# Less of x stored, absolute sums as the bound of W, and the differences of batch 0 spread and loaded back by halves, around a seven-product matrix stage

## The reference, cut to what matters

```python
# x: (2, 1024, 2048), ctx: (2, 2048, 2048), float32
q1 = fake_quant(layernorm(x)); q2 = fake_quant(ctx)        # 8-bit grids
x = x + q1 @ q2                                            # per batch
n = layernorm(x)
w = top-2 router weights of softmax(n @ W_router.T)        # 8 experts
lora = sum over experts of w * ((n @ A_e.T) @ B_e.T) * 2   # rank 16 each
x = x + n @ W_base.T + b_base + lora
```

## Time and profile before

| | |
|---|---|
| median of 3 runs | 1152.16 us (1151.45 to 1152.73) |
| the profiled execution | 1155.63 us |
| its span in the trace | 1153.7 us |
| PE busy | 1005.7 us, 87% |
| DVE busy | 813.3 us, 70% |
| ACT busy | 433.7 us, 38% |
| DMA | 202.41 MB, 175 GB/s over the span |
| chain that ended last, largest | PE L1619 21%; DMA xd<-x_kept 5%; DMA spread<-scratch 4%; DMA w_r<-in_w_n 3% |

### The profile page before, as it was taken

How to read it: one execution, slowest core, us unless ns; L and a number is a source line. 1 busy time by engine, 2 the same in 40 slices (tenths; PEclk the granted TensorE clock), 3 DMA queues, 4 the chain that set the end, 5 groups by cost and what they waited for, 6 DMA issues and landing times.

```text
span 1153.7 us, 15006 instructions
## 1 busy us (share of the span) xinstructions
PE 1005.7 (87%) x5847; PEld 533.5 (46%) x5847; DVE 813.3 (70%) x1503; ACT 433.7 (38%) x428; POOL 18.7 (2%) x40
## 2 busy tenths in 40 slices
PE   0489778699899999898989889998596999999997
PEld 0356455466568943343433434443242444444443
DVE  6667776677663885677777675577339888888985
ACT  3779576676642222222332231123112232223220
POOL 0000000000000000000000000000000000000000
PEclk9899989899899999999999999999797999999999
DMA  8737787767664245466666655531953323323311
GB/s 318 283 140 257 245 274 261 231 219 235 229 219 149 81 130 135 153 198 228 207 219 213 231 180 150 193 96 64 291 192 128 101 91 133 122 80 118 132 47 45
DMA packets 69070, 202.41 MB, mean 175 GB/s; under 512 B 8153, under 2 KB 20489, under 8 KB 62729
## 3 DMA queue, kind: packets, MB, share of 16 engines
q1 hardware_dynamic: 67144, 199.35, 50.2%
q0 software_dynamic: 1280, 2.12, 1.7%
q10 hardware_dynamic: 576, 0.00, 0.0%
HBM read 159.46 MB, written 41.98 MB: 175 GB/s over the span
## 4 chain that ended last, share of the span: by engine, by line
PE 26%; DVE 16%; DMA 16%; issue 6%; ACT 4%; SPq 1%; ACTq 0%; POOL 0%; DVEq 0%; POOLq 0%
PE pair L1619 21%; DMA xd<-x_kept 5%; DMA spread<-scratch 4%; DMA w_r<-in_w_n 3%; DVE w_p L1086 3%; DMA scratch<-w_max 3%; DVE wst L1050 2%; PE pair L1596 2%; PE pair L1575 2%; ACT w_p L703 1%; DVE xd_p L1272 1%; ACT w_r L694 1%; PE pair L1565 1%; SPq L567 1%; DVE sq L1251 1%
## 5 line engine op out<-in xcount | busy, mean ns | idle before, releaser
L1596 PE MATMUL pair<-x2p,w_p 128*128 128x512 f16 x1536 | 345.8, 386 | 0.2
L1460 PE MATMUL pair<-q1T,ctx_q 128*128 128x342 f16 x1536 | 245.4, 323 | 7.4 <-DVE xt L887 7.4
L1596 PEld LDWEIGHTS pair<-x2p,w_p 128*128 128x128 f16 x1536 | 152.6, 99 | 189.1 <-issue 13.3
L1460 PEld LDWEIGHTS pair<-q1T,ctx_q 128*128 128x128 f16 x1536 | 153.6, 101 | 91.6 <-issue 9.0
L1619 PE MATMUL pair<-x2p,w_slot 128*128 128x512 f16 x768 | 173.1, 385 | 3.6 <-DVE u L1336 3.6
L1619 PEld LDWEIGHTS pair<-x2p,w_slot 128*128 128x128 f16 x768 | 76.0, 99 | 97.6 <-issue 5.3
L887 DVE SCALAR_TENSOR_TENSOR xt<-pair,par,xt 128x342 f32<-128x342 f32 (+1 forms) x96 | 54.4, 567 | 64.9 <-DMA xt<-in_xT 59.5
L694 ACT ACTIVATE w_r<-w_r 128x1024 f32<-128x1024 f32 x32 | 33.8, 1057 | 176.2 <-DVE wst L1050 176.2
L1575 PE MATMUL pair<-hwT,b_p 128*128 128x512 f16 x192 | 54.8, 396 | 42.8 <-ACT sq L719 31.8
L631 ACT ACTIVATE ctx_u<-ctx_f,par 128x2048 uint8<-128x2048 f32 x32 | 66.9, 2090 | 63.3 <-DMA ctx_f<-in_ctx 63.1
L1619 PE MATMUL pair<-x2p,x2p 128*128 128x512 f16 x336 | 77.0, 389 | 11.3 <-issue 11.3
(11 more groups left out here) (196 smaller groups left out, 1066.6 us busy)
## 6 DMA issues: line engine op xcount, KB each, us to landing
ctx_f<-in_ctx SPq DMA_DIRECT2D x32, 1024.0 KB, 7.1
rows<-in_x SPq DMA_DIRECT2D x16, 1024.0 KB, 9.0
xt<-in_xT SPq DMA_DIRECT2D x32, 512.0 KB, 4.4
x_kept<-xt SPq DMA_DIRECT2D x32, 512.0 KB, 7.9
w_r<-in_w_n SPq DMA_DIRECT2D x32, 512.0 KB, 5.2
w_f<-in_w_t SPq DMA_DIRECT2D x32, 512.0 KB, 5.1
u<-x_kept SPq DMA_DIRECT2D x64, 256.0 KB, 2.9
outT<-u SPq DMA_DIRECT2D x64, 256.0 KB, 3.2
```

The source lines that it names most:

```text
L1460: ins = M.matmul(bank[at % RING][:, 0:W3], ctx_q[n % NQ][:, k, :], q1T[b][:, k, c * W3:(c + 1) * W3], start=(k == 0), stop=(k == KT - 1))
L1596: M.matmul(base_bank(m)[:, :], w_p[j % 2][wh][:, k, :], x2p[0][:, k, xh, t], start=(k == 0 and q == 0), stop=(k == KT - 1 and q == 2))
```

## The change

1. In the first stage only batch 1's x is stored. The store is issued by ACT, behind `hi_of`, and no longer by SP. `load_xt` waits for a store only where the slot held a block of batch 1 (function `kept` counts them).
2. `out_of` for batch 0 loads no x any more: it builds x again from the two parts in `x2p[0]`, times the scale. It has six passes instead of five, and `load_x` is gone for the 32 plain tiles.
3. The bound of W is a sum of absolute values instead of the largest one. ACT makes it (a second pass over `w_r`), and DVE's `w_max_of` is gone. The buffer of the results, `wst`, is double, and rows of W are loaded one j further ahead: `load_wr(j+3, s)`, `w_sums(j+3)`.
4. The order in an iteration is new: on DVE `w_scale_of(j+1)`, `plain_out(2j-1)`, `w_low(j+1)`, `w_bound_of(j+2)`, `xd_of`, `xd_low`, `plain_out(2j)`; on ACT `lora_of(2j-1)` stands before `w_high(j+1)`.
5. The eight pairs of differences are made at j = 2, 3, 5, 6, 8, 9, 11, 12. The weight sums of the first unit are made at j = 13, 14 and 15 (2, 3 and 2 of them).
6. The last four plain tiles are ordered so that both first halves come before both second halves. The differences come back by halves, on ACT's queue: four DMAs in iteration 15, when the first halves are free, and four after the last tile. The row constants of batch 1 come by halves too.

Core of the diff:

```diff
             def load_xt(n):
                 if n >= 3:
                     sp.wait_ge(sq_done, n - 2)
                     sp.wait_ge(lo_done, n - 2)
-                    sp.wait_ge(x_stored[n % 3], 16 * (n // 3))
+                    if n - 3 >= JT:
+                        sp.wait_ge(x_stored[n % 3], 16 * kept(n - 3))
...
             for j in range(1, JT):
                 if j + 2 < JT:
                     load_b(j + 2)
-                    load_wr(j + 2, 0)
                     load_wf(j + 2)
-                if 2 <= j < 2 + UNITS:
-                    load_xd(j - 2)
-                if j + 2 < JT:
-                    load_wr(j + 2, 1)
+                if j + 3 < JT:
+                    load_wr(j + 3, 0)
+                if j in DIFF_AT:
+                    load_xd(DIFF_AT.index(j))
...
+                if j + 3 < JT:
+                    load_wr(j + 3, 1)
                 store(2 * j - 1)
-                load_x(2 * j + 2)
-                load_x(2 * j + 3)
...
                 A.activation(x2p[b][:, j, 0, :], xt[n % 3][:, :], ACT.Copy, scale=xs[:, b, 0:1]).then_inc(hi_done, 1)
+                if b:
+                    act.dma_start(x_kept[j, :, :], xt[n % 3][:, :]).then_inc(x_stored[n % 3], 16)
...
             def w_sums(j):
 
+                if j >= 2:
+                    act.wait_ge(w_bound, j - 1)
                 for s in range(2):
                     act.wait_ge(wr_landed, 16 * (2 * j + s + 1))
-                    act.wait_ge(w_step, 4 * j + 1 + s)
-                    A.activation(w_r[:, :], w_r[:, :], ACT.Copy, accum_out=wst[:, s, 1:2]).then_inc(w_summed, 1)
+                    A.activation(w_r[:, :], w_r[:, :], ACT.Copy, accum_out=wst[:, j % 2, s, 1:2]).then_inc(w_copied, 1)
+                    act.wait_ge(w_copied, 2 * j + s + 1)
+                    A.activation(w_r[:, :], w_r[:, :], ACT.Abs, accum_out=wst[:, j % 2, s, 0:1]).then_inc(w_summed, 1)
...
             for j in range(1, JT):
+                lora_of(2 * j - 1)
                 if j + 1 < JT:
                     w_high(j + 1)
-                lora_of(2 * j - 1)
...
+                if j == JT - 1:
+                    act.wait_ge(xd_stored, 32 * UNITS)
+                    xd_load(0)
+                    xd_load(3)
+                if j + 3 < JT:
+                    w_sums(j + 3)
+                if j in DIFF_AT:
+                    xd_high(DIFF_AT.index(j))
+                for k in FIRST_MADE.get(j, ()):
+                    s_high(0, k)
                 lora_of(2 * j)
             lora_of(PLAIN - 1)
+            xd_load(1)
+            xd_load(2)
...
+                if b == 0:
...
+                    V.scalar_tensor_tensor(o[:, :], meanB[:, t], wsum[:, j:j + 1], shiftB[:, t], ALU.mult, ALU.add).then_inc(u_step, 1)
+                    dve.wait_ge(u_step, v + 1)
+                    V.scalar_tensor_tensor(o[:, :], x2p[0][:, j, 1, t], xs[:, 0, 1:2], o[:, :], ALU.mult, ALU.add).then_inc(u_step, 1)
+                    dve.wait_ge(u_step, v + 2)
+                    V.scalar_tensor_tensor(o[:, :], x2p[0][:, j, 0, t], xs[:, 0, 1:2], o[:, :], ALU.mult, ALU.add).then_inc(u_step, 1)
```

More of the change, by code:

```diff
@@ L274, in xattn_ffn @@
         nat_out = sem("nat_out")
-        spread_landed = [sem(f"spread_landed{b}") for b in range(BATCH)]
+        spread_landed = [sem(f"spread_landed{b}") for b in range(BATCH + 1)]
         wr_landed = sem("wr_landed")
@@ L371, in xattn_ffn, with kept @@
         OUTS = PLAIN + 4 * UNITS
+        def kept(n):
+            return len([m for m in range(JT, n + 1) if m % 3 == n % 3])
         block = es.enter_context(nc.Block())
@@ L430, in _ @@
                     load_rows(TT + (n + 1) // 2)
-            for n in range(STEPS - 3, STEPS):
-                keep_x(n)
             def load_wr(j, s):
@@ L764, in _, with xd_load @@
                     w_sums(1)
+            def xd_load(s):
+                k0, half, m = ((0, first, PLAIN - 2), (HALF, second, PLAIN), (0, second, PLAIN), (HALF, first, PLAIN - 2))[s]
+                act.wait_ge(g_ready, m)
+                act.wait_ge(u_step, 3 * m)
+                for h in range(2):
+                    act.dma_start(x2p[0][:, k0:k0 + HALF, h, half],
+                                  xd_kept[k0:k0 + HALF, :, h, half].rearrange("j p t -> p j t")).then_inc(xd_back[s], 16)
             w_high(1)
+            w_sums(2)
+            for n in range(STEPS - 3, STEPS):
+                act.wait_ge(x_stored[n % 3], 16 * kept(n))
             lora_of(0)
-            w_sums(2)
+            w_sums(3)
             for j in range(1, JT):
+                lora_of(2 * j - 1)
                 if j + 1 < JT:
                     w_high(j + 1)
-                lora_of(2 * j - 1)
-                if j + 2 < JT:
-                    w_sums(j + 2)
-                if 2 <= j < 2 + UNITS:
-                    xd_high(j - 2)
-                if j == JT - 2:
-                    for k in range(4):
-                        s_high(0, k)
-                if j == JT - 1:
-                    for k in range(4, PRODUCTS):
-                        s_high(0, k)
+                if j == JT - 1:
+                    act.wait_ge(xd_stored, 32 * UNITS)
[3 more added lines that the diff above has]
+                    w_sums(j + 3)
+                if j in DIFF_AT:
+                    xd_high(DIFF_AT.index(j))
+                for k in FIRST_MADE.get(j, ()):
+                    s_high(0, k)
                 lora_of(2 * j)
             lora_of(PLAIN - 1)
+            xd_load(1)
+            xd_load(2)
             for i in range(UNITS):
@@ L1208, in h_split_of @@
             def h_split_of(b):
+                if b:
+                    for n in range(STEPS - 3, STEPS):
+                        dve.wait_ge(x_stored[n % 3], 16 * kept(n))
                 for c in range(NC):
@@ L1221, in _ @@
             h_bound_of(0)
-            w_max_of(1, 0)
             h_scale_of(0)
```

139 lines of the change are left out of this document (64 added, 75 removed).

## The result

| | before | with the change |
|---|---|---|
| median | 1152.45 us (1151.45 to 1152.85) | 1169.81 us (1167.93 to 1171.88) |
| span of the profiled execution | 1153.7 us | 1169.0 us |
| ratio of the medians | | 1.0152 [1.0132, 1.0173] |

The change makes the kernel 1.5% slower. 1156 was forecast, so the sign of the likeliest case holds and the size is short: the sum of the terms was +4 us, the spans differ by 15.3.

What follows compares the result with a forecast made beforehand. PE was taken as nearly always busy, with another chain setting the pace in each of four stretches where it idles. Terms -34 + 53 + 14 - 29 = +4 on median 1152.2 gave 1156 us, range 1136 to 1178.

Steps and rivals of the forecast that it cites:

- the likeliest case: Whole kernel: the forecast itself, slightly slower at 1156 us, own range 1146 to 1166, chance 0.46.
- a: First stage: without batch 0's stores, rounds of transposes take 15.4 us; gain 34 us, ends 20 and 38.
- b: Iterations 2 to 12: the new order forms a loop through `w_r`, 32 or 26 us an iteration; loss 53 us.
- Rival 2: Plain stage: the loop is long because `xd` shares the DMA engines with `w_r`; 1179 us, chance 0.15.
- the row of 7.9: Profile row before the change: the slowest `w_r` landing, 7.9 us, read as having `xd` issued right behind as neighbour.
- Rival 1: Plain stage: the loop is short because `w_r`'s halves land fast, iterations 29.9 and 24.6 us; 1135 us, chance 0.27.
- Rival 3: First stage gives little, rounds staying near 19 us, a gain of 12; 1178 us, chance 0.07.
- rival 4: Plain stage: loads one j ahead work and no loop forms, about 23 us an iteration; 1076 us, chance 0.05.
- c: Iterations 13 to 15: late weights and the reordered last tiles make 66.4 us of 52.8; loss 14, ends 8 and 20.
- d: After the last plain tile: half the differences already in place, stalls fall from 34 to 5 us; gain 29 us.
- The rule on issuing: Behind the plain stage: issuing is usually small beside the DMA; ACT free some 8 us sooner, 3 us less in all.
- The sign: Whole kernel: slower 0.47, faster 0.39, same 0.14; the terms summed to +4 us.

Runs made afterwards that it cites:

- f1: The kernel before with only the store change: batch 0's x not stored, batch 1's stored by ACT, x rebuilt in six passes; 1115.68 us, ratio 0.9652.
- e2: The changed kernel with the two loads of `xd` ahead of the `w_f` loads in SP's list; 1163.71 us, ratio 1.0001.
- e6: The changed kernel with `w_r`'s first half and `xd` ahead of `w_f` on SP, and the second half's sums last on ACT; 1070.14 us.
- g3: The changed kernel with the last four plain tiles in natural order and all eight difference loads on SP behind the last tile; 1174.04 us, ratio 1.0094.
- e7: The changed kernel with all eight loads of differences on SP behind the last plain tile; 1173.27 us, ratio 1.0084.
- f2: The kernel before with the store change, and the first unit's weight sums spread over j = 13, 14 and 15; 1115.26 us, ratio 0.9586.
- g5: The changed kernel with `w_r`'s first half and `xd` ahead of `w_f`, second half's sums last, all eight difference loads on SP behind the last tile; 1079.7 us.

## Why the prediction was right, and where it was not

- **a, first stage: mechanism right, size within its ends.** The middle begins at 309.6 against 347.8, a gain of 38.2 (34 forecast, end 38), and f1 shows it alone. The terms are off one by one. PE's transposes stand at 97.21 and 112.00 and then 15.9 to 16.3 apart where I had 15.4, so the rounds gave 24 us and not 27. The change of batches gave 4.5 for 2. Batch 1 gave 10 for 5: PE doesn't stand there at all (71.00 of 71.00 us busy), and its clock is 1.00 where it was 0.97, which I had not counted. From the start of the middle to iteration 2 another 1.3 us were won, where I had nothing; that is a sum of two parts, since iteration 1 opens 45.8 us sooner (400.80 against 446.57) but takes 27.2 us instead of 20.9. (The 119.3 us of the earlier trace rows are six rounds and not 5.9; it changes nothing.)
- **b, iterations 2 to 12: mechanism right, size short.** 349.5 us and not 334, a loss of 68 and not 53. The step that was mis-sized is the landing of the two halves, "I take 6.2" and "so I take 3.7": over the eight iterations with differences they measured 7.2 and 4.7 us on the mean, 11.9 together and not 9.9. The other steps took 0.5 us less than forecast, so an iteration is 33.5 and not 32; the three without differences are 27.0 and not 26. That is 8 x 1.5 + 3 x 1.0 = 15 us, all of the error. `xd` accounts for 0.7 to 0.9 us of the first half and 0.5 of the second (e2); the other 0.5 of the second stands beside the bound's `spread`, issued 1.2 us before it, and no run takes that neighbour away. A row of the kernel before (3.4, a lone load) was used for a load that has neighbours. Rival 2 (1179) came nearer than the forecast, by 9 us against 14, and `xd` beside the landings, its mechanism, is part of it; the row of 7.9 that it leaned on had `w_f` issued 2.7 us behind the load and `xd` only 4.2 us behind. Rivals 1, 3 and 4 are out: the first wanted 29.9 us an iteration, the third a gain of 12 in the first stage. But rival 4's time can be had: e6 opens the loop and gives 1070.
- **c, iterations 13 to 15: right,** 68.6 against 66.4. The runs split it: 12.6 of the 15.8 us are the order of the last four tiles (68.6 against 56.0 in g3).
- **d, behind the last plain tile: right to the microsecond, and for the wrong reason.** 29.0 was forecast and measured, but not by "half of the differences lies in place": e7 has none of that and is 2 us quicker there. The 352.0 fell, by the runs, through the spread sums (353.3 to 348.6, f1 to f2), through B blocks, x and row constants that go out ahead of the eight loads (348.6 to 337.2, f2 to g3), and through the 12.9 us stall before tile 29, paid for in c (337.2 to 320.9, g3 to e7). These give 32.4, and 1.3 (352.0 to 353.3, before to f1) and 2.1 (e7 to the change) go off again. f2 and g3 differ in their loops too, so the middle step is read off, not isolated. That 29.0 came out to the tenth is luck.
- **The rule on issuing,** weighed there (the Trainium skill, DMA: Bandwidth & Descriptors, "Issuing engines are not separate DMA queues"), would have given 3 us less. The four late issues kept ACT for 10.88 us in the change (12.67 in e6), where I had taken about 10 from the earlier trace rows, so the row and not the rule held. That time sets little: with all eight loads on SP the stretch behind the plain stage is 2.1 us shorter (e7 beside the change) and 4.9 shorter (g5 beside e6).
- **The sign: luck in part.** +4 was a small difference of large terms (-34, +53, +14, -29). With the other three stretches as measured and the loop at its forecast 334 us, the sum would have been zero within 0.3 us. The kernel is slower by the very microseconds by which the landings were mis-sized.

So the change holds one clear gain, less stored (38 to 42 us); a loop in the plain stage that costs 68 us, and 94 less once SP's and ACT's order is mended (e6); an order of tiles that moves a stall; and an early return worth nothing here.

## What to carry to other kernels

When a load is taken further ahead, look at what stands ahead of it in its queue's list: here a load meant to be a block sooner was put behind another's wait for the current block, and one line's place was worth 50 us. Cost such a loop by writing it out from one scale to the next with a landing for each load, and take for each the row with the like neighbours; a load alone is the wrong price. And when a gain is read off as a total, ask what the stretch before it paid: a stall before a boundary can be the same microseconds as the gain behind it.
